# Attention: the weighing of each tile's first probabilities moves from ScalarE to GpSimd

## The reference

```
attn = jax.nn.softmax(jnp.einsum('rbqhd,rbkhd->rbhqk', qe, ke) / D ** 0.5, axis=-1)
o = jnp.einsum('rbhqk,rbkhd->rbqhd', attn, ve)
o = jnp.einsum('rbthd,rbth->bthd', o, rw)
```

## Time and profile before

| | |
|---|---|
| median of 3 runs | 2629.14 us (2626.03 to 2631.78) |
| the profiled execution, its own time | 2631.73 us |
| its span, first to last instruction | 2630.0 us |
| busy over the span | PE 2358.6, DVE 1607.9, POOL 1252.3, ACT 1139.5 us |
| the attention's stretch | from about 375 to 1053 us of the span |
| in 460 to 940 us of it | PE 463.5, DVE 466.9, ACT 447.9, POOL 299.3 us busy of 480 |

### The profile page before, as it was taken

How to read it: one execution, slowest core, us unless ns; L and a number is a source line. 1 busy time by engine, 2 the same in 40 slices (tenths; PEclk the granted TensorE clock), 3 DMA queues, 4 the chain that set the end, 5 groups by cost and what they waited for, 6 DMA issues and landing times. The chain is left out here.

```text
span 2630.0 us, 34349 instructions
## 1 busy us (share of the span) xinstructions
PE 2358.6 (90%) x9812; PEld 1592.2 (61%) x9812; DVE 1607.9 (61%) x2461; ACT 1139.5 (43%) x2390; POOL 1252.3 (48%) x1238
## 2 busy tenths in 40 slices
PE   7999979999999998798999994679899876999999
PEld 5778854555555554674888883435445325788877
DVE  4240229999999998576222223679999996511253
ACT  3323028999999997223222223632223113311121
POOL 0012025666666664656745332269999984111110
PEclk9999989999999998888999996889999998999999
DMA  5245435555555563666334314544444446101021
GB/s 180 85 123 187 120 98 158 168 169 171 160 170 161 170 175 129 209 210 227 134 127 144 117 53 145 196 153 169 174 164 175 175 154 181 64 25 48 16 88 64
DMA packets 267523, 370.58 MB, mean 141 GB/s; under 512 B 36504, under 2 KB 119464, under 8 KB 267408
## 3 DMA queue, kind: packets, MB, share of 16 engines
q1 hardware_dynamic: 228496, 301.25, 36.3%
q0 software_dynamic: 10848, 36.63, 4.1%
q10 hardware_dynamic: 28064, 31.25, 3.6%
HBM read 255.09 MB, written 113.98 MB: 140 GB/s over the span
## 5 line engine op out<-in xcount | busy, mean ns | idle before, releaser
L1068 ACT ACTIVATE attn_probs<-attn_ps_score,attn_nmax 128x512 f32<-128x512 f32 x512 | 342.7, 674 | 2.3 <-DVE attn_nmax L1142 2.3
L2694 PE MATMUL scan_ps_o<-scan_qs,scan_sel 128*128 128x512 f32 x512 | 281.0, 640 | 62.2 <-DVE scan_qs L2635 55.3
L2652 DVE TENSOR_TENSOR_SCAN scan_st<-scan_ps_dec,scan_kv 128x512 f32<-128x512 f32 x256 | 305.7, 1208 | 11.5 <-POOL scan_kv L2601 11.5
L975 PE MATMUL attn_ps_score<-attn_KK,attn_X 64*128 64x512 f32 x512 | 213.9, 465 | 20.6 <-ACT attn_probs L1068 20.2
L1156 DVE SCALAR_TENSOR_TENSOR attn_mixed<-attn_probs,attn_cf,attn_mixed 128x512 f32<-128x512 f32 x256 | 194.3, 759 | 9.1
L2694 PEld LDWEIGHTS scan_ps_o<-scan_qs,scan_sel 128*128 128x128 f32 x512 | 91.1, 197 | 166.2 <-DVE scan_qs L2635 102.2
L2601 POOL TENSOR_TENSOR scan_kv<-gla_vb,gla_gk 128x512 f32<-128x512 f32 x128 | 160.9, 1281 | 40.6 <-POOLq L2122 34.3
L1131 DVE TENSOR_REDUCE attn_raw<-attn_ps_score 128x2 f32<-128x1024 f32 x128 | 156.4, 1222 | 28.9 <-PE attn_ps_score L975 27.8
L975 PE MATMUL attn_ps_score<-attn_KL,attn_X 64*128 64x512 f32 x512 | 172.5, 423 | 0.0
L2601 POOL TENSOR_TENSOR scan_kv<-gla_vb,scan_gk 128x512 f32<-128x512 f32 x128 | 159.5, 1283 | 2.4 <-DVE scan_st L2652 2.4
L975 PE MATMUL attn_ps_score<-attn_KK,attn_Y 64*128 64x512 f32 x512 | 159.9, 399 | 0.8 <-POOL attn_Y L865 0.8
(11 more groups left out here) (557 smaller groups left out, 6442.4 us busy)
## 6 DMA issues: line engine op xcount, KB each, us to landing
gla_vb<-gv SPq DMA_DIRECT2D x256, 256.0 KB
rows_x<-attn_zeros SPq DMA_DIRECT2D x32, 1024.0 KB, 13.6
late<-rows SPq DMA_DIRECT2D x32, 384.0 KB, 9.2
attn_spread<-rows SPq DMA_DIRECT2D x32, 384.0 KB
moe_raw<-in_L_ffn_gating POOLq DMA_DIRECT2D x6, 2048.0 KB, 9.7
moe_xb<-rows_x SPq DMA_DIRECT2D x39, 256.0 KB, 2.7
rows_y<-moe_y ACTq DMA_DIRECT2D x39, 256.0 KB, 2.0
sg<-proj_tile SPq DMA_DIRECT2D x32, 256.0 KB, 2.0
```

Source lines behind the costliest of these rows:

```text
L975: last = nc.tensor.matmul(ps_score[n][:, j, :], weights, y[p][half, :], start=(r == 0), stop=(r == len(terms) - 1))
L1068: nc.scalar.activation(probs[b][:, at_j, :], ps_score[n][:, j, :], ACT.Exp, bias=nmax[b][:, at_j:at_j + 1], accum_out=Z[b][:, at_j:at_j + ...
L2652: V.tensor_tensor_scan(st[r][:, :], ps_dec[n % 2][:, :], kv[r][:, :], 0.0, ALU.mult, ALU.add).then_inc(st_ready, 1)
L2694: nc.tensor.matmul(ps_o[w][:, :], sel[:, P - GPH - GPH * d:2 * P - GPH - GPH * d], qs[i % RING][:, :], start=(d == 0), stop=(d == HALF - 1 ...
```

## The change

`weigh_first` is taken out of ACT's list, four times a unit, and put in POOL's: a `tensor_tensor` multiply in place whose second input is the column `cf[:, 0:1]` repeated 512 times. It still waits for `cf_ready` and still increments `first_ready`; DVE's and PE's lists are as before. In POOL's `step` the weighing of tile n-1 stands behind the operation of the first place and ahead of that of the second place; tile 3 of a unit is weighed in the next unit's step, the last one behind the loop.

```
--- before.py
+++ after.py
@@ -885,6 +885,13 @@
                 pool.wait_ge(kh_ready, u + 1)
                 nc.gpsimd.tensor_tensor(KL[p][:, :], k[p][:, :], KK[p][:, :].bitcast(F32), ALU.subtract).then_inc(kl_ready, 1)
 
+            def weigh_first(u, t):
+
+                b = t % 2
+                pool.wait_ge(cf_ready, u * TT + t + 1)
+                nc.gpsimd.tensor_tensor(probs[b][:, 0, :], probs[b][:, 0, :], cf[b][:, 0:1].to_broadcast([P, T]), ALU.mult
+                                        ).then_inc(first_ready, 1)
+
             def masked_sums(u, t):
 
                 b, n = t % 2, u * TT + t
@@ -895,12 +902,17 @@
                 nc.gpsimd.tensor_tensor(Z[b][:, 2:4], Z[b][:, 2:4], tz[b][:, :], ALU.add).then_inc(z_ready, 1)
 
             def step(i, p, u, first):
+                first_tile = first and p == 0
                 if left(u) >= 1:
-                    beside_first_maxima(u, 0, first and p == 0)
+                    beside_first_maxima(u, 0, first_tile)
                     choose(i + p, 1 - p, u + 1, 1)
+                if not first_tile:
+                    weigh_first(u - 1, 3)
+                if left(u) >= 1:
                     beside_maxima(u, 0)
                     choose(i + p, 1 - p, u + 1, 2)
                 masked_sums(u, 0)
+                weigh_first(u, 0)
                 if left(u) >= 1:
                     beside_maxima(u, 1)
                     low_keys(i + p, 1 - p, u + 1)
@@ -908,6 +920,7 @@
                 if not first:
                     beside_first_maxima(u, 2, False)
                     gate(i - 1, p, u - 2)
+                weigh_first(u, 1)
                 if left(u) >= 2:
                     beside_maxima(u, 2)
                     choose(i + 1, p, u + 2, 0)
@@ -915,6 +928,8 @@
                 if left(u) >= 1:
                     beside_first_maxima(u, 3, False)
                     rest(1 - p, u + 1, SHARED)
+                weigh_first(u, 2)
+                if left(u) >= 1:
                     beside_maxima(u, 3)
                     rest(1 - p, u + 1, AB)
                 masked_sums(u, 3)
@@ -932,6 +947,7 @@
                 nc.gpsimd.memset(o[p][:, :], 0.0).then_inc(o_free[p], 16)
             choose(0, 1, 1, 0)
             every_unit(pool, step)
+            weigh_first(U - 1, 3)
             for p in two:
                 gate(U // 2 - 1, p, U - 2 + p)
 
@@ -1071,12 +1087,6 @@
                         act.wait_ge(probs_ready, (u * TT + t) * 4 + 2)
                         nc.scalar.activation(ez[b][:, :], nmax[b][:, 2:4], ACT.Exp).then_inc(ez_ready, 1)
 
-            def weigh_first(u, t):
-
-                b = t % 2
-                act.wait_ge(cf_ready, u * TT + t + 1)
-                nc.scalar.activation(probs[b][:, 0, :], probs[b][:, 0, :], ACT.Copy, scale=cf[b][:, 0:1]).then_inc(first_ready, 1)
-
             def take_turned(u, t, p, first):
                 act.wait_ge(tr_done, u * TT + t + 1)
                 if t == 0 and not first:
@@ -1093,21 +1103,17 @@
                     keys(i + p, 1 - p, u + 1, first)
                 if not first_pair:
                     lift(u - 2, isinstance(u, int) and u == 2)
-                weigh_first(u, 0)
                 softmax(u, 1, first)
                 if not first:
                     take_turned(u - 1, 3, 1 - p, False)
                 if left(u) >= 1:
                     take(1 - p, u + 1, SHARED, first)
-                weigh_first(u, 1)
                 softmax(u, 2, first)
                 take_turned(u, 0, p, first_pair)
                 if left(u) >= 1:
                     take(1 - p, u + 1, AB, first)
-                weigh_first(u, 2)
                 softmax(u, 3, first)
                 take_turned(u, 1, p, first_pair)
-                weigh_first(u, 3)
 
             keys(0, 0, 0, True)
             for n in (SHARED, AB):
```

More of the change, by code:

```diff
@@ L1072, in softmax @@
                         nc.scalar.activation(ez[b][:, :], nmax[b][:, 2:4], ACT.Exp).then_inc(ez_ready, 1)
[L1074 to L1078, removed]
             def take_turned(u, t, p, first):
```

## The result

The changed kernel takes 2739.91 us (median of 4 runs, 2736.31 to 2742.55) against 2628.86 us before (4 runs, 2626.03 to 2631.78): a ratio of 1.0418, 95% interval 1.0404 to 1.0433. It is 111 us slower.

What follows compares the result with a forecast made beforehand. DVE's work was taken to fill the tile, with the mixture setting the price: 128 x (6.47 - 5.15) = 169 us, less 5 for units outside the loop, giving 2793 us, range 2760 to 2822.

Steps and rivals of the forecast that it cites:

- What bounds the kernel: In the attention, DVE's own work fills 5.06 us a tile without a hole; POOL operations hold up its mixture.
- Step 1: On ACT, 128 weighings of 722 ns go; worth nothing on DVE's chain, though exponentials come 0.63 us or more earlier.
- Step 2: On POOL, 128 weighings of 128 x 512 come, taken at 1.27 us each.
- My bounds: Limits for the weighing's length on POOL: 0.52 us from one-input operations, 1.49 us from the slowest two-input one.
- Step 3: POOL's weighing runs from 703.38 to 704.65, so DVE's mixture, possible at 704.32, waits at least 0.33 us.
- the sign that I had named: In the changed profile, DVE idle some 0.3 us before each mixture, released by the weighing on POOL.
- Step 4: POOL's second-place operation, queued behind the weighing, holds DVE's mixture: a tile of 6.47 us, or 6.37 in the other order.
- Steps 5 and 6: All four tiles pay, the first place costs nothing; masked sums, PE's and ACT's work stay hidden within 6.47 us.
- The cheap weighing: Rival: POOL's weighing takes only 0.52 us, a tile 5.72 us, 2702 us in all; chance 8 in 100.
- The other rivals: Weighing alone costs, 2669 us (5 in 100); dearer tile, 2815 to 2830 (13 in 100); ACT's relief real, 2619 (2 in 100).

## Why the prediction was off

**What bounds the kernel: right.** DVE's own work and the hold-ups of its mixture fill the tile; with the weighing gone altogether only 5 us are gained.

**Step 1 (ScalarE's relief is worth nothing): right but for a little.** Without any weighing the undisturbed tile shown is 0.08 us shorter. PE's AB scores ended at 706.56, right ahead of the maxima at 706.60. In the changed kernel the maxima start 1.46 us after the second mixture operation (705.70 to 707.16), where I had used 1.51.

**Step 2 (the weighing's length): this is the term that failed.** I took 1.27 us "since the column is still read as a second stream"; it measured 1.04. The run with a full second input gave 1.27 and cost 29 us more. That is over half of the 53 us by which the forecast was too high, but not all of it: with the length alone put right the forecast is 2764 us, just inside the range. The smaller terms below, another 0.18 us a tile or 23 us, took it out. My bounds, 0.52 and 1.49, held the value, but the range was cut well inside them; the sentence that at 1.0 us the time would be 2758 already stood outside my range of 2760 to 2822.

**Step 3 (the weighing is late by at least 0.33 us): wrong with it.** It starts 0.08 us after `cf`, not 0.16, and ends 0.02 us after the mixture could start. I had read 0.16 from one row, of an operation that waited for another signal; a start 0.1 us earlier was in the forecast's own range. What failed with the length is the lateness: the mixture starts 0.05 us late instead of 0.33. So the sign that I had named, some 0.3 us of idle time before each mixture, did not appear either (0.8 us in 79).

**Step 4 (the displaced operation holds the mixture): right.** It starts ahead of the mixture (0.04 us before the weighing's end, I had 0), takes 1.28 us, and the mixture's first operation ends 0.54 later; 0.55 was read from the earlier trace rows. In the whole trace of the changed kernel it is 0.55 in all 121 tiles in which that operation is held (0.545 to 0.554). The late second place on its own made 95 of the 111 us. Read to the letter, the Trainium skill, "SBUF — State Buffer" (Who interferes with whom; the words "fully blocks until the first finishes" stand in its section "Summary: rules for kernel authors"), would have put that end at 0.74, an estimate with the operation's own duration; the tile of the changed kernel shows 0.54 and that of the earlier trace rows 0.55. That the waiting operation blocks until the other is over agrees with the trace.

**Steps 5 and 6: right.** All four tiles of a unit pay (6.06 to 6.11 us each in the loop), the first place costs nothing, and 1/Z never waited in the window.

The sum, for the tile shown: 6.47 forecast, less 0.23 (length), 0.08 (start), 0.04 (overlap), 0.05 (next maxima) and 0.01 net for the rest, is 6.06 as measured. 128 x 0.41 = 52 us: 2793 - 52 = 2741, against 2739.91.

**The rivals.** The cheap weighing came true in part, at 1.04 between its 0.52 and my 1.27. The other rivals did not: the granted clock stayed at 1.00 from 460 to 940 us with PE at 412.0 / 480 = 86% busy.

## What to carry to other kernels

Before moving an operation to GpSimd, lay its interval and that of everything queued behind it over VectorE's operations with two SBUF inputs; what is displaced can cost more than what is moved. An engine that is 97% busy in both profiles may still have lost a sixth of its pace, so compare the count and the mean of each group, not the busy share or the waits. Where an operation's form is not in the trace, let the range reach to both bounds of its price: here the one term that was not read from a row of its own form carried over half of the error.

## What the runs showed of the hardware that I had not expected

A GpSimd product of 128 x 512 takes 1.04 us when its second input is a repeated column (1038 to 1041 ns over 128 of them) and 1.27 us when it is a full tile of zeros (1265 mean over 128); nothing else was changed between the two.

In the changed kernel a GpSimd operation whose waits are met starts about 0.04 us before the end of the one ahead of it, while a VectorE operation that waits for that end starts 0.03 us after it. In all 121 held tiles the displaced operation started first. Where the mixture's first operation starts first, its second is held instead: the earlier trace rows, and in the run with only the second place late one tile in every turn of the loop (13 durations, 1.65 to 1.66 us). So in these traces the order of the starts decides which one waits.
